# A graph network's layer on one core: sums of node ranges in two banks, and fewer signals from PE

## The reference

```python
msg_in = concatenate([x[src], x[dst]])
h = relu(msg_in @ Wm1 + bm1)
h = relu(h @ Wm2 + bm2)
messages = h @ Wm3 + bm3
agg = segment_sum(messages, dst) / clip(count, 1)[:, None]
upd = relu(concatenate([x, agg]) @ Wn1 + bn1) @ Wn2 + bn2
out = layernorm(x + (x + upd))
```

## Time and profile before

| | us |
|---|---|
| median of 3 runs | 1459.47 (1455.62 to 1460.34) |
| the profiled execution | 1460.04 |
| its span, first to last instruction | 1458.2 |
| PE busy | 1278.1 (88%) |
| PE's weight loads | 1205.2 (83%) |
| DVE busy | 976.7 (67%) |
| ACT busy | 746.7 (51%) |
| POOL busy | 778.1 (53%) |
| mean granted clock of PE | 0.974 |

### The profile page before, as it was taken

The page is one execution under the profiler, slowest core; times in us unless marked ns, Lnnn a source line. Parts: engine busy times, 40 slices in busy tenths (PEclk is TensorE's granted clock), DMA queues, the critical chain, the costliest instruction groups (busy, mean ns, idle before and its releaser), DMA issues.

```text
span 1458.2 us, 37162 instructions
## 1 busy us (share of the span) xinstructions
PE 1278.1 (88%) x9807; PEld 1205.2 (83%) x9808; DVE 976.7 (67%) x2120; ACT 746.7 (51%) x1409; POOL 778.1 (53%) x810
## 2 busy tenths in 40 slices
PE   7969889898988888899888889898889988899797
PEld 6758788887988888888888888888888888888686
DVE  5746666666666666666676667767777777777575
ACT  4525544555454545455454455555455554545486
POOL 1156666666665666656666565666565655654000
PEclk9989999999999999989999999999999999999899
DMA  9854444444444444445454444455544444544023
GB/s 285 288 194 143 143 148 147 147 143 143 146 148 142 143 146 147 140 141 146 141 144 147 134 147 144 139 145 147 143 140 146 146 137 147 146 129 134 8 59 90
DMA packets 158504, 211.26 MB, mean 145 GB/s; under 512 B 24234, under 2 KB 127106, under 8 KB 158467
## 3 DMA queue, kind: packets, MB, share of 16 engines
q1 hardware_dynamic: 119818, 107.51, 25.6%
q0 software_dynamic: 37536, 102.55, 22.6%
q10 hardware_dynamic: 1112, 0.79, 0.2%
HBM read 187.96 MB, written 22.80 MB: 145 GB/s over the span
## 4 chain that ended last, share of the span: by engine, by line
PE 55%; issue 17%; another core or an unknown queue 7%; DVE 7%; ACT 6%; DVEq 6%; DMA 1%; ACTq 0%; POOL 0%
PE bank L1194 23%; PE bank L1129 7%; PE bank L1163 6%; PE bank L1142 5%; PE bank L1144 4%; DVEq L323 3%; PE bank L1227 2%; PE bank L1084 2%; DVE onehot L873 2%; ACT h L597 2%; ACT h_hi L592 2%; ACT bank L600 2%; PE bank L1240 1%; PE bank L1105 1%
## 5 line engine op out<-in xcount | busy, mean ns | idle before, releaser
L510 POOL DMA_INDIRECT a_edge<-a_table,src_idx x782 | 759.8, 972 | 499.5 <-remote 193.5
L1194 PE MATMUL bank<-w,h 128*128 128x256 f32 x4692 | 642.3, 285 | 24.2 <-issue 23.8
L1194 PEld LDWEIGHTS bank<-w,h 128*128 128x128 f32 x4692 | 597.8, 192 | 31.9 <-issue 31.7
L592 ACT ACTIVATE h_hi<-bank 128x512 fp32r<-128x512 f32 x391 | 235.4, 602 | 388.5 <-remote 195.3
L932 DVE SCALAR_TENSOR_TENSOR h_lo<-bank,h_hi 128x512 fp32r<-128x512 f32 x391 | 267.5, 684 | 178.7 <-issue 125.0
L944 DVE SCALAR_TENSOR_TENSOR h<-bank,h 128x512 fp32r<-128x512 f32 x391 | 268.8, 687 | 158.6 <-issue 98.9
L597 ACT ACTIVATE h<-bank 128x512 fp32r<-128x512 f32 x391 | 233.4, 597 | 244.1 <-PE bank L1129 115.1
L1142 PE MATMUL bank<-h_hi,onehot 128*128 128x258 f32 x878 | 244.3, 299 | 95.6 <-DVE onehot L873 40.6
L1142 PEld LDWEIGHTS bank<-h_hi,onehot 128*128 128x128 f32 x878 | 168.1, 192 | 121.0 <-issue 71.1
L1163 PE MATMUL bank<-ident,a_edge 128*128 128x128 f32 x1564 | 242.5, 278 | 18.1 <-issue 10.7
L600 ACT COPY bank<-b_bc 128x512 f32<-128x512 f32 x391 | 234.0, 598 | 0.0
(11 more groups left out here) (142 smaller groups left out, 551.7 us busy)
## 6 DMA issues: line engine op xcount, KB each, us to landing
b_win<-b_table SPq DMA_DIRECT2D x391, 128.0 KB
rel<-rel_dram SPq DMA_DIRECT2D x196, 128.0 KB
a_edge<-a_table,src_idx POOLq DMA_INDIRECT x782
a_table<-work SPq DMA_DIRECT2D x12, 512.0 KB, 3.4
b_table<-work SPq DMA_DIRECT2D x4, 1024.0 KB, 5.4
b_table<-h SPq DMA_DIRECT2D x4, 1024.0 KB, 5.2
b_table<-a_edge SPq DMA_DIRECT2D x4, 1024.0 KB, 5.0
f_x<-in_x SPq DMA_DIRECT2D x12, 256.0 KB, 5.4
```

Source lines behind the costliest of these rows:

```text
L510: pool.indirect_dma_start(a_edge[:, b % R * TB + t, :], None, a_table, bass.IndirectOffsetOnAxis(ap=src_idx[:, b * TB + t:b * TB + t + 1], ...
L592: act.activation(h2_hi[:, (k - AHEAD - 1) % U, :, 0:H], bank[H2[(k - AHEAD - 1) % U]][:, :].rearrange("p (t h) -> p t h", t=TB), ACT.Relu) ...
L1194: ins = pe.matmul(to, h1[:, j, a, h * EB + t * P:h * EB + (t + 1) * P], w2[:, b, h, :], start=False, stop=(a == 1 and h == KH - 1), skip_g ...
```

## The change

- The loop's sums go into two banks in turn, halves of one tensor `sums`; PE and DVE keep the offsets of the `own` and the `other` bank in registers. Where a block reaches into the next window and the next block begins there, PE writes its second part into the other bank, beginning it anew, and swaps; DVE adds the own bank to agg after the signal of the product in the same step, and swaps. Other ends of windows (the last one here) take a longer way with waits on both sides. s_clr is gone, and with it PE's wait in every step.
- PE signals after the expansion and after the product; s_ta and s_sg of each block are gone. POOL waits for s_ex in place of s_ta.
- DVE's order in a step: one-hot of block k - 3, h2_lo of block k - 3, transposed one-hot of block k + 2 (after the wait for h1_hi of block k), h1_lo of block k, then the end of a window, and the second one-hot, now of block k - 3.
- In the head DVE makes a by adding b1, held on all partitions, to PE's product; ACT makes both halves of x @ Wn1. PE's matmuls with b1 go, ACT no longer copies a.
- The words carry two more bits; making them takes DVE five more small instructions (not shown).

```diff
--- before.py
+++ after.py
...
-        bank = [ctx.enter_context(nc.psum_tensor(f"bank{i}", [P, 512], F32)) for i in range(8)]
-        SUM, SUM_MORE = 4, 5
+        bank = [ctx.enter_context(nc.psum_tensor(f"bank{i}", [P, 512], F32)) for i in range(4)]
+        sums = ctx.enter_context(nc.psum_tensor("sums", [P, 1024], F32))
+        bank += [sums[:, 0:512], sums[:, 512:1024]]
+        bank += [ctx.enter_context(nc.psum_tensor(f"bank{i}", [P, 512], F32)) for i in range(6, 8)]
+        SUM = 4
...
-                    pool.wait_ge(s_ta, b - R + 1)
+                    pool.wait_ge(s_ex, b - R + 1)
...
+            act.dma_start(b1_bc, bm1.partition_broadcast(P)).then_inc(s_w, 16)
...
-                    act.copy(a_out[:, k % 2, 2 * q:2 * q + m, :],
-                             bank[2 + q][:, 0:m * H].rearrange("p (w h) -> p w h", h=H)).then_inc(s_ac, 1)
...
+                    for h, to in enumerate((hx[0], hx_more)):
+                        act.activation(to[:, (g - 1) * GW * P:((g - 1) * GW + n) * P], bank[6 + h][:, 0:n * P],
+                                       ACT.Identity, bias=bn1_col[:, h:h + 1]).then_inc(s_hxa, 1)
...
+                    dve.tensor_tensor(a_out[:, (g - 1) % 2, 2 * q:2 * q + m, :],
+                                      bank[2 + q][:, 0:m * H].rearrange("p (w h) -> p w h", h=H),
+                                      b1_bc.unsqueeze(1).to_broadcast([P, m, H]), ALU.add
+                                      ).then_inc(s_ac, 1)
...
-                    dve.wait_ge(s_hx, g)
-                    dve.tensor_scalar(hx_more[:, (g - 1) * GW * P:((g - 1) * GW + n) * P], bank[7][:, 0:n * P],
-                                      bn1_col[:, 1:2], None, ALU.add).then_inc(s_hxd, 1)
...
-            def add_sums(b, w):
+            def bank_at(which):
+                return sums[:, bass.ds(within(dve.snap(which), 0, 512), HC)]
+            def add_sums(which, w):
                 dve.reg_add(added, added, 1)
-                sums = agg[:, bass.ds(w * HC, HC)]
-                return dve.tensor_tensor(sums, bank[b][:, 0:HC], sums, ALU.add).then_inc(s_add, 1)
-            def finish_sums(i, k, word):
-                dve.wait_ge(s_sg, i * U + (k + 1))
-                add_sums(SUM, within(word & 63, 0, NW - 1))
-                dve.wait_ge(s_add, added)
-                dve.memset(bank[SUM][:, 0:HC], 0.0).then_inc(s_add, 1)
-                dve.reg_add(added, added, 1)
-                dve.wait_ge(s_add, added)
-                dve.nop().then_inc(s_fin, 1)
-            def finish_further(i, k, word):
+                in_agg = agg[:, bass.ds(w * HC, HC)]
+                dve.tensor_tensor(in_agg, bank_at(which), in_agg, ALU.add).then_inc(s_add, 1)
+            def end_window(i, k, word):
                 w = word & 63
-                further = (word >> 14) & 63
-                with dve.If(further > 0):
-                    dve.wait_ge(s_sgm, more)
-                    add_sums(SUM_MORE, within(w + 1, 1, NW - 1))
-                    with dve.If(further > 1):
-                        with dve.Fori(2, within(further, 2, NW - 1) + 1) as j:
-                            dve.wait_ge(s_add, added)
-                            make_further_onehot(i, k, j)
-                            dve.wait_ge(s_sgm, more)
-                            add_sums(SUM_MORE, within(w + j, 1, NW - 1))
+                with dve.If((word & (3 * 2**6)) > 0):
+                    with dve.If((word & 2**7) > 0):
+                        dve.wait_ge(s_w2, i * U + (k + BACK - AHEAD + 1))
+                        add_sums(own, within(w, 0, NW - 1))
+                        dve.reg_mov(swap, own)
+                        dve.reg_mov(own, other)
+                        dve.reg_mov(other, swap)
+                    with dve.If((word & 2**6) > 0):
+                        dve.reg_add(left, left, 1)
+                        dve.wait_ge(s_sg, left)
+                        add_sums(own, within(w, 0, NW - 1))
+                        dve.wait_ge(s_add, added)
+                        no_row = ident[:, 0:1].to_broadcast([P, HC])
+                        dve.tensor_tensor(bank_at(own), no_row, no_row, ALU.subtract
+                                          ).then_inc(s_add, 1)
+                        dve.reg_add(added, added, 1)
+                        further = (word >> 15) & 63
+                        with dve.If(further > 0):
+                            with dve.Fori(1, within(further, 1, NW - 1) + 1) as j:
+                                make_further_onehot(i, k, j)
+                                dve.wait_ge(s_sgm, more)
+                                dve.wait_ge(s_add, added)
+                                add_sums(other, within(w + j, 1, NW - 1))
                     dve.wait_ge(s_add, added)
                     dve.nop().then_inc(s_fin, 1)
...
+                        make_onehot(j, i, k - AHEAD - 1, 0, s_oh)
                         dve.wait_ge(s_h2h, i * U + (k - AHEAD))
                         dve.scalar_tensor_tensor(h2_lo[:, j, :, :],
                                                  bank[H2[j]][:, :].rearrange("p (t h) -> p t h", t=TB),
                                                  0.0, h2_hi[:, j, :, 0:H].bitcast(F32),
                                                  ALU.max, ALU.subtract).then_inc(s_h2l, 1)
+                    if there(i, k):
+                        dve.wait_ge(s_h1h, i * U + (k + 1))
+                        if there(i, k + 2):
+                            if (k + 2) % 2 == 0:
+                                dve.wait_ge(s_rc[(k + 2) // 2 % RC], (i + (k + 2) // U) * 16 + 16)
+                            make_onehot_t(k + 2)
+                        dve.scalar_tensor_tensor(h1[:, k % U, 1, :], bank[k % 2][:, :], 0.0,
+                                                 h1[:, k % U, 0, :].bitcast(F32), ALU.max, ALU.subtract
+                                                 ).then_inc(s_h1l, 1)
                     with dve.If(flag > 0):
                         word = load_words(dve, words_dve, i * U + k, 1, DVE_TOP)[0]
                         if there(i, k - BACK):
-                            with dve.If((word & 64) > 0):
-                                finish_sums(i, k - BACK, word)
-                    dve.nop().then_inc(s_clr, 1)
-                    if there(i, k):
-                        dve.wait_ge(s_h1h, i * U + (k + 1))
-                        dve.scalar_tensor_tensor(h1[:, k % U, 1, :], bank[k % 2][:, :], 0.0,
-                                                 h1[:, k % U, 0, :].bitcast(F32), ALU.max, ALU.subtract
-                                                 ).then_inc(s_h1l, 1)
-                    if there(i, k - AHEAD - 1):
-                        make_onehot((k - AHEAD - 1) % U, i, k - AHEAD - 1, 0, s_oh)
-                    with dve.If(flag > 0):
-                        word = load_words(dve, words_dve, i * U + k, 1, DVE_TOP)[0]
-                        if there(i, k - BACK):
-                            finish_further(i, k - BACK, word)
-                        if there(i, k - BACK + 1):
-                            with dve.If(word > 2**20 - 1):
-                                make_further_onehot(i, k - BACK + 1, 1)
+                            end_window(i, k - BACK, word)
+                        if there(i, k - AHEAD - 1):
+                            with dve.If(word > 2**21 - 1):
+                                make_further_onehot(i, k - AHEAD - 1, 1)
                         if there(i, k) and there(i, k + 1):
-                            with dve.If((word & (127 * 2**7)) > 0):
+                            with dve.If((word & (127 * 2**8)) > 0):
                                 far_onehots_t(k + 1, word)
-                    if there(i, k) and there(i, k + 2):
-                        if (k + 2) % 2 == 0:
-                            dve.wait_ge(s_rc[(k + 2) // 2 % RC], (i + (k + 2) // U) * 16 + 16)
-                        make_onehot_t(k + 2)
...
-                    pe.matmul(bank[4 + q][:, 0:m * H], ones2[:, :], b1_rows[:, 0:m * H], start=True, stop=False,
-                              skip_group_check=True)
...
-            def sum_further(k):
-                pe.reg_add(more, more, 1)
-                pe.wait_ge(s_ohm, more)
-                sum_segments(bank[SUM_MORE], FURTHER, k, True).then_inc(s_sgm, 1)
+            def end_window(k, word):
+                with pe.If(word > 2**13 - 1):
+                    pe.wait_ge(s_fin, ended)
+                    pe.reg_add(ended, ended, 1)
+                    with pe.If((word & 2**13) > 0):
+                        pe.matmul(bank_at(other)[:, 0:2], ident[:, :], ident[:, 0:2], start=True, stop=True,
+                                  skip_group_check=True).then_inc(s_sg, 1)
+                    further = (word >> 7) & 63
+                    with pe.If(further > 0):
+                        with pe.Fori(1, within(further, 1, NW - 1) + 1):
+                            pe.reg_add(more, more, 1)
```

(19 more changed lines are left out.)

120 lines of the change are left out of this document (70 added, 50 removed).

## The result

The changed kernel takes 1478.8 us (median of 4 runs, 1475.18 to 1483.06) against 1459.12 for the kernel before on the same chip: ratio 1.014, 95% interval 1.0106 to 1.0174. It is 1.4% slower; the forecast was 1310.

The account below looks back on a forecast made before the run. The prediction took PE's late notices, let through one at a time during gathers, to bound the loop. From 1460.04 us, -150 for signals, other parts 0 or included, less 0.6, gave 1309, say 1310; eight in ten 1235 to 1430.

Parts of the forecast that it names:

- The signals: Loop: two PE notices a block in place of four shorten the step from 3.204 to 2.82 us, -150 us.
- passage: Loop: while POOL issues gathers, one PE notice at a time gets through, some 1.55 us apart.
- rival A: Loop: notices pass as before, the round through POOL sets 3.11 us; -41 us, 1418 us; chance 0.28.
- the Trainium skill's rule: PE's matmul increments serialize at about 26 ns each; two fewer give an estimated 20 us, 1439 by it alone.
- PE's sequencer: Loop: register work for the bank address, taken as 0; each 0.1 us a block beyond the cover costs 39 us.
- s_clr and the two banks: Window crossings: removes up to 63 us of PE's idle time, counted inside the 2.82 us step.
- the prediction's own fallback: Where the loop's period stays at 3.1 us, s_clr and the two banks are worth some 25 us.
- DVE's order and the added wait: Loop: later h1_lo just fits; DVE's wait for the product at crossings costs 0 to 19 us.
- rival C: Crossings: DVE's new wait delays h1_lo and stops PE; slower, +49 us, 1508 us; chance 0.07.
- Head: Before the loop: PE's b1 matmuls go, DVE gets adds; -10 to +11 us, taken as 0.
- Tail: After the loop: untouched, no change in time.
- Rival B: Loop: every notice finds a passage, PE's own step of 2.57 to 2.62 us rules; 1215 to 1235 us; chance 0.07.

Follow-up runs that it names:

- e1_head: The kernel before with only the head's change (b1 added by DVE, x @ Wn1 made by ACT): ratio 1.0023 on a chip without holds.
- e3b_fast: The changed kernel with PE's window-end code in line, usual case first, no loop, two branches less: ratio 0.9926 to before, notices held.
- a2_after: The changed kernel as it is, against the kernel before, on a chip that doesn't hold notices: 1302.3 us, ratio 1.0396.
- a1_after: The changed kernel as it is, against the kernel before, on a chip that holds notices: 1461.4 us, ratio 1.0155.
- e5b_half_gathers: The changed kernel with one gather a block in place of two, on a chip that holds notices: 1300.7 us, ratio 0.9035 to before.

## Why the prediction was wrong

*The signals: the step that failed.* I sized it at -150 us: each notice has a passage of its own, so two fewer let the block go from 3.14 to 2.82 us. Measured: the step away from crossings is 3.11 before and 3.13 after, the whole loop 20 us longer in place of 150 shorter, and undoing the two notices (with POOL's wait where it was) makes the kernel 1.4% faster. What holds a notice is the gathers under way, 1.5 us each, however many notices there are. The rows for that were on the table. In the earlier trace rows two gathers go with 3.15 us from first gather to first gather, 1.57 each. The four in a row, from 218 us to the answer at 224.23, are 6.2 us, 1.55 each. I took those four as evidence for the passages and against rival A, without dividing. The last sentence of the prediction names this as what would make it fall (delay by something else than number).

*Rival A* had the pace right: a step of 3.10, and pauses as the rule. Its reason, the round through POOL, doesn't hold for the rows of four, which have the same pace with half of the rounds; and its 1418 us took a gain of 41 us that the crossings didn't give. *By the Trainium skill's rule* in "TensorE: Matmul & The Clock Gate" (per-tile semaphore tail) two increments fewer should have given an estimated 20 us; the traces don't bear this out here: without holds four notices and two differ by nothing that can be measured (1.0389, 1.0397 and 1.0396), with holds by 1.4% in the other direction.

*PE's sequencer: the second step that failed.* I put it at 0, "beside matmuls that run on without gaps", and gave 39 us for each 0.1 us a block. The cost sits not in each block but at 48 crossings, where the sequencer has two more branches and a loop to get through and PE has nothing queued. On the chip without holds PE's stops in the crossing's step (starts further apart than 0.12 us) are 36.3 us before the second half of the sums and 16.1 before the product, 1.1 us a crossing; the step is 4.34 us against 3.17 of the kernel before's loop (in e1_head): 55 us. With holds 33 us, by e3b_fast.

*s_clr and the two banks.* I took out up to 63 us of PE's waits, and they did go (waits after). The time went over to PE's own path, which had been running under them: PE's idle time in the loop is 139.4 us before and 140.1 after. In e3b_fast, where that is short, the change's loop is worth 0.7% against before, with its slower head; in the prediction's own fallback this was 25 us, 1.7%.

*DVE's order and the added wait.* The order fits: PE waits 0.6 and 0.5 us in all for h1's lo part. DVE does stand for the late product, 75 us over 36 crossings, up to 3.5 us, and PE doesn't feel it: the steps behind a crossing are 2.81, 2.64 and 2.63. So *rival C* had the sign and not the cause: its place was PE before transposes for h1_lo, where PE stands 0.5 us in all.

*Head*: 2.9 us, within the -10 to +11. *Tail*: 2.5 us shorter in the profiled executions, untouched as said. *Rival B* is the pace of the other sort of chip away from crossings (2.58 us in a2_after).

In sum, of the 20 us: about 20 by two notices fewer, 33 by PE's branches, 3 by the head, less what the banks and the early one-hot give back, 36 us by difference and not measured by themselves. The first two aren't independent: both act on the lower clock, and with short branches two notices leave only 10 us at it. What stays open is how two notices fewer, or POOL's later wait, bring the clock down.

## What to carry to other kernels

When a delay is explained by a count (of signals, of instructions), divide it by each of the candidate causes in every stretch that shows it, the one that seems to support you above all. Code that a rare case runs on the sequencer of the engine that sets the pace is paid as soon as that engine has nothing queued (0.80 of 1.83 us a crossing here, and 1.39 where notices are held): test the usual case first, without a loop. And measure on more than one chip: a ratio may be 1.0396 on one and 1.0155 on the next.

## What the runs showed of the hardware

Two sorts of chip, told apart by this kernel: 1252 against 1438 to 1459 us. On the second, PE's semaphore notices are held while GpSimd issues indirect DMAs, 1.5 us for each, with 64 rows as with 128. PE also stops there in the middle of products with no wait written (56.1 us in 134 stops on record, 4.1 in 24 without holds); that this comes of too much unanswered work is a guess. Why chips differ so isn't settled by these runs.

The hold isn't only of notices. Where notices are held, register and branch instructions of the sequencers of PE and SP, with no wait in their records, take some 0.7 us now and then in place of 0.03 to 0.2: over 0.4 us 35 times on PE and 153 times on SP in the loop of the changed kernel on record, never on either in a2_after. It goes with the gathers too: with one a block (e5b_half_gathers, on a chip that holds) it is never on PE and 4 times on SP.

The same branches stop PE for longer where notices are held. In the median the sequencer takes 1.83 us from the branch on the flag to the next matmul on either sort of chip (649.29 to 651.12 us in a1_after, 560.94 to 562.77 in a2_after); the mean is 2.07 on record and 1.98 in a1_after, by the held instructions, against 1.85 in a2_after. And without holds the sequencer is there some 0.7 us before PE's first matmul of the sums, with holds 0.2 us or not at all; both having just stood there would explain that. So PE's stop is 1.39 us from start to start with holds and 0.80 without.
